# The two layer norms that follow attention take one set of statistics, and the rows of the second are made one tile at a time between the softmax tiles

## The chip, the cores and the metric

The kernel runs on one core of a Trainium2 chip. The metric is the device time of one execution in microseconds (us); less is better. TensorE (PE) does the matrix products and transposes, VectorE (DVE), ScalarE (ACT) and GpSimd (POOL) the elementwise work, and SyncE (SP) issues most of the DMA transfers. Each engine runs its own list of instructions in order; the lists meet only in semaphores.

## The reference, cut to what matters

The input is 4 images of 256 channels and 1024 positions (tokens). Three stages follow each other: a group norm with self-attention, an attention between tokens with residual MLPs, and a mixture of experts (8 experts, 2 for each token).

```python
x = _L0_conv_ref(x, ...)                  # group norm, softmax attention, + xn
t = _to_tokens(x)                         # 4 x 1024 tokens x 256
t = t + _L1_attn_ref(_ln_t(t), ...)       # "t1" below: tokens + second attention
t = t + _L1_ffn_ref(_ln_t(t), ...)        # the experts

def _L1_ffn_ref(x, ...):                  # x = _ln_t(t1), "x2" below
    x_norm = _layernorm(x, ln_g, ln_b)    # "xf" below: norm of a norm, times g, plus b
    ...                                   # gate, top 2 of 8, experts on x_norm
    return x + out
```

Both norms take mean and variance over the 256 channels of a token and add 1e-5 to the variance. The result is t1 + x2 + out, so two things leave this part for every token: the row t1 + x2, to which the experts' outputs are added in memory, and the row xf, from which the gate is computed and which the experts gather.

## The kernel before

All fp32 products are made in three passes of a high and a low part (`three`, L1545), so most of TensorE's time lies in that one helper line. The tile is 128 tokens x 256 channels; an image has 8 tiles (NT).

The function `image(b, first, last)` exists once for each engine. For image b it runs: eight parts of projections (`project`), then softmax 1 over 8 tiles, then a phase R of 24 parts (`R`: kinds "u", "p", "v", the MLPs and projections of the second attention), then softmax 2 over 8 tiles. Image 0 is written out, images 1 and 2 are a hardware loop (`Fori`), image 3 is written out again. In softmax 1 TensorE does in step i: `turn1(i)` (8 transposes of the exponentials), `scores(i + 2)`, `mix1(i - 1)`. VectorE does in step i: `lo1(i)` (low part of the transposed exponentials), `max1(i + 2)`, `out1(i - 1)` (result row, its own norm statistics), `norm1(i - 2)`. ScalarE does `hi1(i)` and `exp1(i + 2)`. GpSimd raises the variance of each tile to the power -0.5 (`first_norm`).

The norms after the second attention of image b - 1, the "tail", have no phase of their own: their pieces are put between the softmax 1 steps of image b, and behind image 3 they stand alone. The pieces before:

- `tail_add` (DVE, L1200): tok = tok + attention, from PSUM.
- `tail_stats(b, which, h)` (DVE, L1211 to L1216) for four tiles (half h) of norm `which`: bn_stats, bn_aggr, then variance + eps.
- `scale` (POOL, L586, L611, L612): power -0.5 of four values, mean times that, times -1.
- `tail_norm` (ACT, L749): four activations that write x2 (norm 0) or xf (norm 1).
- `stream` (POOL, L618): r_out = tok + x2; `affine` (POOL, L623, L625): xf times g_row, plus b_row, four tiles an instruction. For the last image two DVE instructions for each half do the affine part (L1435, L1438).

They are placed by the tables `ACT_TAIL = {1: (0, 1), 3: (1, 0), 4: (1, 1)}` and `DVE_TAIL = {2: (1, 0), 3: (1, 1)}` (step: norm, half), and by `image` for norm 0. In ScalarE's list the first tail piece stands ahead of `hi1(0)` and `exp1(1)`. SP sends r_out and xf to memory (L479, L482), and behind them in its queue loads the next image into xn (L471). In phase R TensorE transposes xf at part 10 (`gate_turn`, L1578) and computes the gate at parts 13 to 16 (`gate`, L1587).

After image 3, DVE, ACT, POOL, SP and PE all wait for each other (`ends`) before the routing begins (L995 on DVE, L666 on POOL). SP joins when both transfers of the last image have landed.

Of the kernel before, what the change touches and what calls it, by code (L numbers as in the profile page):

```python
# [29 lines left out]
P = 128  # L30
# [20 lines left out]
def hybrid_block_kernel(nc, x, q_w, k_w, v_w, oT, q_b, v_b, out_b, gn, W1, W2T, a_qk, a_vT, Wout,  # L51
# [31 lines left out]
    with ctx:  # L83
# [19 lines left out]
        minus_one = sb("minus_one", [P, 8])  # L103
# [43 lines left out]
        tl_bn = bs("tl_bn", [P, 2, NT, 6])  # L147
        tl_mv = bs("tl_mv", [P, 2, NT, 2])
        tl_eps = bs("tl_eps", [P, 2, NT])
        tl_r = bs("tl_r", [P, 2, NT])  # L150
        tl_mr = bs("tl_mr", [P, 2, NT])
        tl_nb = bs("tl_nb", [P, 2, NT])
# [18 lines left out]
        x2 = sb("x2", [P, NT, C], F32, here)  # L171
# [154 lines left out]
        x2_done = signal("x2_done")  # L326
        xf_norm = signal("xf_norm")
# [80 lines left out]
        ACT_TAIL = {1: (0, 1), 3: (1, 0), 4: (1, 1)}  # L408
        DVE_TAIL = {2: (1, 0), 3: (1, 1)}
# [27 lines left out]
        def _(sp):  # L437
# [123 lines left out]
        def _(pool):  # L561
# [11 lines left out]
            make(g.memset(minus_one[:, :], -1.0))  # L573
# [22 lines left out]
            TL_OWN = 8 + 2  # L596

            def last_norms(b, between_norms, affines=True):

                n = [0]  # L600

                def own_step(ins):
                    n[0] += 1
                    ins.then_inc(tl_own, 1)
                    pool.wait_ge(tl_own, at(b, TL_OWN, n[0]))

                def scale(which, h):
                    c = slice(4 * h, 4 * h + 4)
                    pool.wait_ge(tl_in, at(b, 4, 2 * which + h + 1))
                    own_step(rsqrt(tl_r[:, which, c], tl_eps[:, which, c]))  # L610
                    own_step(g.tensor_tensor(tl_mr[:, which, c], tl_mv[:, which, c, 0], tl_r[:, which, c], ALU.mult))  # L611
                    g.tensor_tensor(tl_nb[:, which, c], tl_mr[:, which, c], minus_one[:, 0:4],  # L612
                                    ALU.mult).then_inc(tl_out, 1)

                def stream(h):
                    c = slice(4 * h, 4 * h + 4)
                    pool.wait_ge(x2_done, at(b, 2, h + 1))
                    g.tensor_tensor(r_out[:, c, :], tok[:, c, :], x2[:, c, :], ALU.add).then_inc(r_ready, 1)  # L618

                def affine(h):  # L620
                    c = slice(4 * h, 4 * h + 4)
                    pool.wait_ge(xf_norm, at(b, 2, h + 1))
                    own_step(g.tensor_tensor(xf[:, c, :], xf[:, c, :],  # L623
                                             g_row[:, :].unsqueeze(1).to_broadcast((P, 4, C)), ALU.mult))
                    g.tensor_tensor(xf[:, c, :], xf[:, c, :],  # L625
                                    b_row[:, :].unsqueeze(1).to_broadcast((P, 4, C)), ALU.add).then_inc(xf_ready, 1)

                scale(0, 0)
                scale(0, 1)
                if affines:  # L630
                    stream(0)
                    stream(1)
                between_norms(0)
                between_norms(1)
                scale(1, 0)
                between_norms(2)
                scale(1, 1)
                if not affines:
                    stream(0)
                    stream(1)  # L640
                else:
                    affine(0)
                    between_norms(3)
                    affine(1)
                assert n[0] == TL_OWN or not affines

            def image(b, first, last):
                if not first:
                    last_norms(b - 1, lambda i: first_norm(b, i))
                for i in range(0 if first else 4, NT):  # L650
                    first_norm(b, i)
# [8 lines left out]
            last_norms(B - 1, lambda i: None, affines=False)  # L660
# [64 lines left out]
        def _(act):  # L725
# [18 lines left out]
            def tail_norm(b, which, h):  # L744

                src, dst, ready = ((tok, x2, x2_done), (x2, xf, xf_norm))[which]
                act.wait_ge(tl_out, at(b, 4, 2 * which + h + 1))
                for j in range(4 * h, 4 * h + 4):
                    ins = a.activation(dst[:, j, :], src[:, j, :], ACT.Identity,  # L749
                                       bias=tl_nb[:, which, j:j + 1], scale=tl_r[:, which, j:j + 1])  # L750
                ins.then_inc(ready, 1)
# [6 lines left out]
            def image(b, first, last):  # L758
# [44 lines left out]
                else:  # L803
                    tail_norm(b - 1, 0, 0)
# [67 lines left out]
            for which in range(2):  # L872
                for h in range(2):
                    tail_norm(B - 1, which, h)
            for h in range(2):
                gate_columns(B - 1, h)
            act.wait_ge(xf_col, 2 * B)
# [1028 lines left out]
CONSTANTS = 8  # L1906
# [44 lines left out]
```

## Time and profile before

| | |
|---|---|
| median of 3 runs | 1255.43 us (1252.72 to 1256.72) |
| the profiled execution | 1255.06 us, of which the span of the trace is 1253.2 us |
| PE busy | 1154.5 us (92%) |
| DVE / ACT / POOL busy | 822.1 / 545.5 / 342.7 us |
| images, their softmaxes and phases R | 0 to 693 us |
| tail of image 3 alone, gate, top 2 | 693 to 728 us |
| routing | 728 to 776 us |
| experts and output | 776 to 1253 us |

A row of the timeline gives start, length, engine, line, operation, output and inputs with their shapes, and in brackets how long the engine stood idle before it and what ended that. Instructions of an engine overlap by a little, so the start of the next one can lie before the end of the one before. Matmul ends are modelled.

### The profile page before, as it was taken

Reading aid. Unit: us, or ns where it says so; the run is one execution under the profiler, and the core shown is the slowest. Engines: PE = TensorE matmul, PEld = TensorE weight load, DVE = VectorE, ACT = ScalarE, POOL = GpSimd, SP = SyncE. Lnnn points to the kernel's source line nnn. Section 1 sums busy time; section 2 is a strip of 40 time slices with the busy share of each in tenths; the row PEclk is TensorE's granted clock in tenths of the full one; section 3 lists DMA queues with packets and bytes.
Section 4 is the critical chain, followed back from the end, with each engine's and each line's share of the span. In section 5 each row is a group of like instructions: output and inputs, shape, how many; then the busy total and the mean of one; then the engine's idle time right before and its main releaser. Section 6 shows DMA issues by size and latency. Waiting matters only on the chain.

```text
span 1253.2 us, 25051 instructions
## 1 busy us (share of the span) xinstructions
PE 1154.5 (92%) x8118; PEld 1075.5 (86%) x8119; DVE 822.1 (66%) x1883; ACT 545.5 (44%) x995; POOL 342.7 (27%) x352
## 2 busy tenths in 40 slices
PE   6999999999999999999999335999999999999993
PEld 5897998988988889989888234899999999999992
DVE  4675475954667744768436777796797678856651
ACT  2533445432435334454334313674574556644431
POOL 0010002500004300025000325355455455555440
PEclk9999999999999999999999658899999999999996
DMA  5000000200001100011000133363563547533238
GB/s 164 1 4 31 1 1 1 69 34 1 1 2 35 68 1 1 1 35 35 1 1 1 62 112 106 104 198 53 170 201 52 155 90 216 147 59 54 55 46 273
DMA packets 66207, 82.70 MB, mean 66 GB/s; under 512 B 11105, under 2 KB 56545, under 8 KB 66145
## 3 DMA queue, kind: packets, MB, share of 16 engines
q1 hardware_dynamic: 52128, 63.48, 15.6%
q0 software_dynamic: 14016, 18.37, 8.2%
q8 instruction: 42, 0.69, 0.2%
q14 instruction: 21, 0.16, 0.0%
HBM read 60.85 MB, written 22.02 MB: 66 GB/s over the span
## 4 chain that ended last, share of the span: by engine, by line
PE 81%; DVE 8%; DMA 4%; issue 3%; SPq 1%; ACT 1%; DVEq 1%; POOL 0%; ACTq 0%; POOLq 0%
PE ps L1545 74%; PE ps L1625 2%; DMA w1r<-in_w 2%; PE ps L1587 1%; PE ps L1835 1%; PE ps L1558 1%; DMA rows<-acc_rows 1%; DVE w2s L1466 1%; DVE hs L1512 1%; DVE one_hot L1095 1%; DVE pick_hi L1103 1%; PE ps L1578 1%; PE ps L1634 1%; PE ps L1647 1%; DVE pick_lo L1098 1%
## 5 line engine op out<-in xcount | busy, mean ns | idle before, releaser
L1545 PE MATMUL ps<-xt,w1s 128*128 128x256 f32 x1746 | 257.8, 284 | 1.5 <-DVE xt L1476 1.5
L1545 PE MATMUL ps<-w2s,hs 128*128 128x256 f32 x1728 | 251.1, 280 | 2.8 <-DVE hs L1514 2.7
L1545 PEld LDWEIGHTS ps<-xt,w1s 128*128 128x128 f32 x1746 | 227.7, 190 | 2.1 <-DVE xt L1476 1.9
L1545 PEld LDWEIGHTS ps<-w2s,hs 128*128 128x128 f32 x1728 | 223.6, 188 | 4.2 <-issue 4.1
L944 ACT ACTIVATE h<-ps,b1t 128x256 f32<-128x256 f32 x288 | 137.3, 477 | 114.0 <-PE ps L1545 79.0
L704 POOL DMA_INDIRECT acc_rows<-y_w,now_s x72 | 119.8, 1665 | 166.2 <-issue 155.1
L1512 DVE CAST hs<-h 128x256 fp32r<-128x256 f32 x288 | 91.0, 316 | 71.0 <-ACT h L944 35.9
L1514 DVE TENSOR_TENSOR hs<-h,hs 128x256 fp32r<-128x256 f32 x288 | 123.0, 427 | 9.9
L1545 PE MATMUL ps<-xs,wh 128*128 128x512 f32 x384 | 123.1, 401 | 1.5 <-issue 1.5
L586 POOL TENSOR_TENSOR tl_r<-tl_eps,minus_half 128x4 f32<-128x4 f32 x16 | 16.2, 1014 | 350.8 <-DVE tl_eps L1216 350.8
L691 POOL DMA_INDIRECT xg<-xf_rows,now_g x76 | 93.2, 1226 | 47.3 <-POOL now_g L687 34.7
L1545 PE MATMUL ps<-vs,pr 128*128 128x256 f32 x768 | 98.1, 283 | 0.0
L1545 PEld LDWEIGHTS ps<-vk,pr 128*128 128x128 f32 x768 | 94.0, 188 | 3.2 <-DVE pr L1357 0.8
L1545 PE MATMUL ps<-xs,qs 128*128 128x512 f32 x384 | 95.5, 397 | 0.0
L1545 PE MATMUL ps<-vk,pr 128*128 128x256 f32 x768 | 94.8, 279 | 0.6 <-DVE pr L1357 0.6
L1545 PE MATMUL ps<-qs,ks 128*128 128x512 f32 x384 | 92.3, 391 | 0.0
L1545 PEld LDWEIGHTS ps<-vs,pr 128*128 128x128 f32 x768 | 92.2, 188 | 0.0
L1352 DVE TENSOR_REDUCE neg_max<-ps 128x1 f32<-128x1024 f32 x32 | 39.2, 1225 | 79.7 <-PE ps L1545 79.7
L1545 PEld LDWEIGHTS ps<-xs,wh 128*128 128x128 f32 x384 | 69.7, 189 | 16.0 <-issue 1.7
L1545 PEld LDWEIGHTS ps<-qs,ks 128*128 128x128 f32 x384 | 70.1, 188 | 13.5
L1545 PEld LDWEIGHTS ps<-xs,qs 128*128 128x128 f32 x384 | 69.8, 188 | 13.6
L1545 PE MATMUL ps<-xs,wl 128*128 128x512 f32 x192 | 76.2, 397 | 0.0
(213 smaller groups left out, 1871.5 us busy)
## 6 DMA issues: line engine op xcount, KB each, us to landing
w1r<-in_w SPq DMA_DIRECT2D x16, 1024.0 KB, 5.1
w2r<-in_w SPq DMA_DIRECT2D x16, 1024.0 KB, 8.9
b2t<-in_b SPq DMA_DIRECT2D x36, 128.0 KB, 2.9
xn<-in_x SPq DMA_DIRECT2D x4, 1024.0 KB, 4.9
acc_rows<-r_out SPq DMA_DIRECT2D x4, 1024.0 KB, 4.5
xf_rows<-xf SPq DMA_DIRECT2D x4, 1024.0 KB, 4.9
rows<-acc_rows SPq DMA_DIRECT2D x8, 512.0 KB, 7.4
out_tokens<-cols_out SPq DMA_DIRECT2D x8, 512.0 KB, 9.0
```

The lines of the kernel that those rows point to most:

```text
L586: return g.tensor_tensor(dst, src, minus_half[:, 0:src.shape[1]], ALU.pow)
L691: g.indirect_dma_start(out=xg[:, n, h, :], out_offset=None, in_=xf_d, in_offset=bass.IndirectOffsetOnAxis(ap=now_g[:, n, h:h + 1], axis=0) ...
L704: g.indirect_dma_start(out=acc_d, out_offset=bass.IndirectOffsetOnAxis(ap=now_s[:, n, h:h + 1], axis=0), in_=y_w[:, n, h, :], in_offset=No ...
L944: a.activation(h32[:, gi % 4, :], bank(gi % 4, STEP), ACT.Gelu, bias=b1t[:, n, f:f + 1]).then_inc(h_act, 1)
L1095: v.tensor_tensor(one_hot[:, j, :], iota[:, 0:COLS].unsqueeze(1).to_broadcast((P, PICK, COLS)), hi_f[:, k, t].unsqueeze(2).to_broadcast((P ...
L1098: v.tensor_tensor(pick_lo[:, j, :], iota[:, :].unsqueeze(1).to_broadcast((P, PICK, P)), lo_f[:, k, t].unsqueeze(2).to_broadcast((P, PICK, P)),
L1103: v.tensor_tensor(pick_hi[:, j, 1, :], one_hot[:, j, :], top_w[:, k, t].unsqueeze(2).to_broadcast((P, PICK, COLS)), ALU.mult).then_inc(pic ...
L1352: v.tensor_reduce(neg_max[:, i:i + 1], bank(2 * (i % 2), count=2), AXX, ALU.max, negate=True).then_inc(s2_max, 1)
L1512: v.tensor_copy(hs[0][:, f, :], h32[:, gi % 4, :]).then_inc(h_hi, 1)
L1514: v.tensor_tensor(hs[1][:, f, :], h32[:, gi % 4, :], hs[0][:, f, :].bitcast(F32), ALU.subtract).then_inc(h_lo, 1)
L1545: ins = t.matmul(out, left[l], right[r], start=first and n == 0, stop=last and n == 2, **more)
L1625: ins = t.transpose(bank(4, count=2)[:, j * P:(j + 1) * P], prob[:, i % 2, j * P:(j + 1) * P], ident[:, :])
```

## The change

The statistics of the second norm are worked out from those of the first. With variance v, the norm of the norm scales (t1 - mean) by 1/sqrt(v + eps) and again by 1/sqrt(v/(v + eps) + eps); the product is (v(1 + eps) + eps^2)^-0.5. So both reciprocal roots come from one GpSimd instruction over 8 values (`tail_scales`). `tail_stats` runs for one norm only and has two more small instructions, `tail_xf` makes one tile of xf on DVE in two instructions, and `tail_rows` makes r_out = t1 * (1 + r) - mean * r on ACT in one activation for each tile. `tail_add` writes t1, a tile of its own. x2, `stream`, `affine` and the second round of statistics are gone.

```diff
-        ACT_TAIL = {1: (0, 1), 3: (1, 0), 4: (1, 1)}
-        DVE_TAIL = {2: (1, 0), 3: (1, 1)}
+        DVE_TAIL = {1: (0,), 2: (1,), 3: (2,), 4: (3,), 5: (4,), 6: (5,), 7: (6, 7)}
...
# SP
-                sp.wait_ge(xf_ready, at(b, 2, 2))
+                sp.wait_ge(xf_ready, at(b, NT, NT))
...
# POOL
+            def tail_scales(b, h):
+                c = slice(4 * h, 4 * h + 4)
+                pool.wait_ge(tl_in, at(b, 2, h + 1))
+                g.tensor_tensor(tl_r[:, :, c], tl_eps[:, :, c],
+                                minus_half[:, :].rearrange("p (k t) -> p k t", k=2), ALU.pow).then_inc(tl_own, 1)
+                pool.wait_ge(tl_own, at(b, 2, h + 1))
+                g.tensor_tensor(tl_nb[:, c], tl_nm[:, c], tl_r[:, 0, c], ALU.mult).then_inc(tl_out, 1)
+                g.tensor_tensor(tl_s[:, c], tl_r[:, 0, c], ones[:, 0:4], ALU.add).then_inc(tl_out, 1)
...
# ACT
+            def tail_rows(b, h):
+                act.wait_ge(tl_out, at(b, 4, 2 * h + 2))
+                if not (isinstance(b, int) and b == 0):
+                    act.wait_ge(tok_out, at(b, 16, 0))
                 for j in range(4 * h, 4 * h + 4):
+                    ins = a.activation(r_out[:, j, :], t1[:, j, :], ACT.Identity,
+                                       bias=tl_nb[:, j:j + 1], scale=tl_s[:, j:j + 1])
+                ins.then_inc(r_ready, 1)
...
-                    tail_norm(b - 1, 0, 0)
+                    tail_rows(b - 1, 0)
                     hi1(0)
                 exp1(1)
...
-                    if not first and i in ACT_TAIL:
-                        tail_norm(b - 1, *ACT_TAIL[i])
+                    if not first and i == 1:
+                        tail_rows(b - 1, 1)
...
             act.wait_ge(xf_out, (B - 1) * 16)
-            for which in range(2):
-                for h in range(2):
-                    tail_norm(B - 1, which, h)
             for h in range(2):
                 gate_columns(B - 1, h)
+            for h in range(2):
+                tail_rows(B - 1, h)
...
# DVE
+                v.tensor_scalar(tl_eps[:, 1, cs], tl_mv[:, cs, 1], 1.0 + LN_EPS, LN_EPS * LN_EPS,
+                                ALU.mult, ALU.add)
+                v.tensor_scalar(tl_nm[:, cs], tl_mv[:, cs, 0], -1.0, None, ALU.mult)
+                v.tensor_scalar(tl_eps[:, 0, cs], tl_mv[:, cs, 1], LN_EPS, None, ALU.add).then_inc(tl_in, 1)
+            def tail_xf(b, j):
+                if j % 4 == 0:
+                    dve.wait_ge(tl_own, at(b, 2, j // 4 + 1))
+                if j == 0 and not (isinstance(b, int) and b == 0):
+                    dve.wait_ge(xf_out, at(b, 16, 0))
+                step(v.scalar_tensor_tensor(xf[:, j, :], t1[:, j, :], tl_mv[:, j, 0:1], g_row[:, :],
+                                            ALU.subtract, ALU.mult))
+                settle()
+                v.scalar_tensor_tensor(xf[:, j, :], xf[:, j, :], tl_r[:, 1, j:j + 1], b_row[:, :],
+                                       ALU.mult, ALU.add).then_inc(xf_ready, 1)
...
                 if not first:
                     lo1(0)
-                    tail_stats(b - 1, 0, 1)
...
                     if i + 2 < NT:
                         max1(i + 2)
+                    if not first and i == 0:
+                        tail_stats(b - 1, 1)
                     if i >= 1:
                         out1(i - 1)
                     if i >= 2:
                         norm1(i - 2)
                     if not first and i in DVE_TAIL:
-                        tail_stats(b - 1, *DVE_TAIL[i])
+                        for j in DVE_TAIL[i]:
+                            tail_xf(b - 1, j)
...
                 if not first:
-                    w(xf_ready, 2, 0)
                     w(tok_out, 16, 0)
...
# DVE behind image 3
             tail_add(B - 1, 0)
-            tail_stats(B - 1, 0, 0)
+            tail_stats(B - 1, 0)
             tail_add(B - 1, 1)
-            tail_stats(B - 1, 0, 1)
-            tail_stats(B - 1, 1, 0)
+            tail_stats(B - 1, 1)
+            for j in range(NT):
+                tail_xf(B - 1, j)
             tops(range(0, NT))
-            tail_stats(B - 1, 1, 1)
             tops(range(NT, 2 * NT))
...
```

The wait of `out1(0)` for r_ready is gone too. In TensorE's list only the counts of `xf_ready` differ.

## Rows read from the trace of the kernel before

**Rows 1.** The page, its part 4: chain that ended last, shares by engine.
```profile
PE 81%; DVE 8%; DMA 4%; issue 3%; SPq 1%; ACT 1%; DVEq 1%; POOL 0%; ACTq 0%; POOLq 0%
```

**Rows 2.** Waits of PE over the span: us in total, times, longest.
```profile
PE ps L1578 <- DVE xf L1438: 21.9, 2, 21.5
```

**Rows 3.** Timeline, image 1, the start of softmax 1.
```profile
203.33 1.02 POOL L586 TENSOR_TENSOR tl_r<-tl_eps,minus_half 128x4 f32<-128x4 f32 x1 [70.81 <-DVE tl_eps L1216]
204.95 2.08 ACT L749 ACTIVATE x<-tok,tl_nb,tl_r 128x256 f32<-128x256 f32 x4 [1.39 <-POOL tl_nb L612]
...
207.96 1.23 DVE L1250 TENSOR_TENSOR pr<-ps,pr 128x1024 fp32r<-128x1024 f32 x1 [0.99 <-ACT pr L785]
...
209.33 1.07 PE L1625 MATMUL ps<-ident,prob 128*128 128x128 f32 x8
```

**Rows 4.** The power instruction by tile: ns min/median/max, first and last start.
```profile
L586 POOL TENSOR_TENSOR ln_r<-ln_eps,minus_half x32: 549/646/663, 55.4 to 593.2; 128x1 f32<-128x1 f32 x32
L586 POOL TENSOR_TENSOR tl_r<-tl_eps,minus_half x16: 1007/1017/1020, 203.3 to 706.4; 128x4 f32<-128x4 f32 x16
```

**Rows 5.** DVE's groups by line and shape, 200 to 720 us: busy, mean ns.
```profile
L1369 DVE SCALAR_TENSOR_TENSOR vk<-v,row_inv,vk 128x256 fp32r<-128x256 f32 x24 | 11.6, 484 | 0.9
```

**Rows 6.** Timeline, image 1, the end of softmax 1 and the start of phase R.
```profile
243.01 0.42 DVE L1259 TENSOR_TENSOR tok<-ps,o_row 128x256 f32<-128x256 f32 x1 [0.37 <-PE ps L1545]
...
246.92 0.42 DVE L1259 TENSOR_TENSOR tok<-ps,o_row 128x256 f32<-128x256 f32 x1
...
248.65 0.41 DVE L1273 TENSOR_SCALAR tn<-tok,ln_mv,ln_r 128x256 f32<-128x256 f32 x1
...
248.96 1.22 DVE L1279 TENSOR_TENSOR xs<-ps,xs 128x1024 fp32r<-128x1024 f32 x1
...
250.10 1.22 DVE L1250 TENSOR_TENSOR pr<-ps,pr 128x1024 fp32r<-128x1024 f32 x1
...
254.72 0.42 DVE L1259 TENSOR_TENSOR tok<-ps,o_row 128x256 f32<-128x256 f32 x1
...
259.05 0.69 DVE L1335 TENSOR_TENSOR us<-prob,us 128x512 fp32r<-128x512 f32 x1
...
260.14 0.63 PE L1545 MATMUL ps<-xs,wh 128*128 128x512 f32 x2
```

**Rows 7.** The chain that ended last, in order of time: start, us, what.
```profile
275.19 1.75 PE ps L1578 x16
```

**Rows 8.** A DMA issue of the page (KB, us to landing); one us by windows.
```profile
acc_rows<-r_out SPq DMA_DIRECT2D x4, 1024.0 KB, 4.5
...
221.00:222.00 1.00, 1.00 (x11) 1.00 (x10) 1.00 (x3) 0.00 (x0) 0.39 (x1) 1.00 1.04 346
```

**Rows 9.** Timeline behind image 3 (two rows); then one group by tile.
```profile
707.91 5.63 POOL L618 TENSOR_TENSOR r_out<-tok,x 128x1024 f32<-128x1024 f32 x2
...
708.00 3.34 DVE L1435 TENSOR_TENSOR xf<-xf,g_row 128x1024 f32<-128x1024 f32 x1
...
L687 POOL COPY now_g<-gather_at x38: 184/748/1239, 775.3 to 1203.6; 128x2 int32 x34, 128x2 int32<-128x2 int32 x4
```

**Rows 10.** Timeline, the tail behind image 3, until the routing begins.
```profile
693.39 1.29 DVE L1200 TENSOR_TENSOR tok<-ps,tok 128x512 f32<-128x512 f32 x2 [3.92 <-PE ps L1545]
...
696.65 1.28 DVE L1200 TENSOR_TENSOR tok<-ps,tok 128x512 f32<-128x512 f32 x2
...
699.82 0.17 DVE L1216 TENSOR_SCALAR tl_eps<-tl_mv 128x4 f32<-128x4 f32 x1
...
713.63 0.37 SPq L479 DMA_DIRECT2D acc_rows<-r_out  x1
...
717.07 1.97 PE L1578 MATMUL ps<-ident,xf 128*128 128x128 f32 x8 [0.36 <-DVE xf L1438]
...
719.08 1.01 ACT L755 COPY xfT<-ps 128x1024 f32<-128x1024 f32 x1 [1.32 <-PE ps L1578]
...
728.13 0.24 POOL L666 IOTA iota_i<- 128x128 int32 x1 [14.59 <-DVEq L1445]
```

More of the change, by code:

```diff
@@ L145, in hybrid_block_kernel @@
         ln_r = bs("ln_r", [P, NT])
-        tl_bn = bs("tl_bn", [P, 2, NT, 6])
-        tl_mv = bs("tl_mv", [P, 2, NT, 2])
+        tl_bn = bs("tl_bn", [P, NT, 6])
+        tl_mv = bs("tl_mv", [P, NT, 2])
+        tl_nm = bs("tl_nm", [P, NT])
         tl_eps = bs("tl_eps", [P, 2, NT])
         tl_r = bs("tl_r", [P, 2, NT])
-        tl_mr = bs("tl_mr", [P, 2, NT])
-        tl_nb = bs("tl_nb", [P, 2, NT])
+        tl_nb = bs("tl_nb", [P, NT])
+        tl_s = bs("tl_s", [P, NT])
         xf = bs("xf", [P, NT, C])
@@ L170, in hybrid_block_kernel @@
         here.close()
-        x2 = sb("x2", [P, NT, C], F32, here)
+        t1 = sb("t1", [P, NT, C], F32, here)
         r_out = sb("r_out", [P, NT, C], F32, here)
@@ L572, in _ @@
             make(g.memset(minus_half[:, :], -0.5))
-            make(g.memset(minus_one[:, :], -1.0))
             pool.wait_ge(c_made, made[0])
@@ L594, in first_norm @@
                 rsqrt(ln_r[:, i:i + 1], ln_eps[:, i:i + 1]).then_inc(ln_out, 1)
[L596 to L645, printed above, removed]
@@ L647, in image @@
             def image(b, first, last):
                 if not first:
-                    last_norms(b - 1, lambda i: first_norm(b, i))
-                for i in range(0 if first else 4, NT):
+                    for h in range(2):
+                        tail_scales(b - 1, h)
+                for i in range(NT):
                     first_norm(b, i)
@@ L659, in _ @@
             image(B - 1, False, True)
-            last_norms(B - 1, lambda i: None, affines=False)
+            for h in range(2):
+                tail_scales(B - 1, h)
             pool.wait_ge(tl_out, 4 * B)
@@ L871, in _ @@
             act.wait_ge(xf_out, (B - 1) * 16)
-            for which in range(2):
-                for h in range(2):
-                    tail_norm(B - 1, which, h)
             for h in range(2):
                 gate_columns(B - 1, h)
+            for h in range(2):
+                tail_rows(B - 1, h)
             act.wait_ge(xf_col, 2 * B)
@@ L1198, in tail_add, with tail_stats @@
                 for m in (2 * h, 2 * h + 1):
-                    tile = tok[:, 2 * m:2 * m + 2, :].rearrange("p j c -> p (j c)")
-                    ins = v.tensor_tensor(tile, bank(4 + m), tile, ALU.add)
+                    j = slice(2 * m, 2 * m + 2)
+                    ins = v.tensor_tensor(t1[:, j, :].rearrange("p j c -> p (j c)"), bank(4 + m),
+                                          tok[:, j, :].rearrange("p j c -> p (j c)"), ALU.add)
                 ins.then_inc(added2, 1)
-            def tail_stats(b, which, h):
-                if which:
-                    dve.wait_ge(x2_done, at(b, 2, h + 1))
-                else:
-                    dve.wait_ge(added2, at(b, 2, h + 1))
-                src = (tok, x2)[which]
+            def tail_stats(b, h):
+                dve.wait_ge(added2, at(b, 2, h + 1))
@@ L1209, in tail_stats @@
                 c = range(4 * h, 4 * h + 4)
+                cs = slice(4 * h, 4 * h + 4)
                 for i in c:
-                    step(v.bn_stats(tl_bn[:, which, i, :], src[:, i, :]))
+                    step(v.bn_stats(tl_bn[:, i, :], t1[:, i, :]))
                 settle_aggr()
                 for i in c:
-                    step(v.bn_aggr(tl_mv[:, which, i, :], tl_bn[:, which, i, :]))
+                    step(v.bn_aggr(tl_mv[:, i, :], tl_bn[:, i, :]))
                 settle()
-                v.tensor_scalar(tl_eps[:, which, 4 * h:4 * h + 4], tl_mv[:, which, 4 * h:4 * h + 4, 1], LN_EPS,
-                                None, ALU.add).then_inc(tl_in, 1)
+                v.tensor_scalar(tl_eps[:, 1, cs], tl_mv[:, cs, 1], 1.0 + LN_EPS, LN_EPS * LN_EPS,
+                                ALU.mult, ALU.add)
@@ L1256, in out1 @@
                     w(av_mm, NT, i + 1)
-                    if i == 0 and not first:
-                        w(r_ready, 2, 0)
                     step(v.tensor_tensor(tok[:, i, :], bank(6 + i % 2)[:, C:2 * C], o_row[:, :], ALU.add))
@@ L1292, in image @@
                 if not first:
-                    tail_stats(b - 1, 0, 0)
+                    tail_stats(b - 1, 0)
                 project_lo(6)
@@ L1903, in _ @@
                 ins.then_inc(o_mm, 1)
-CONSTANTS = 8
-OWN_IMAGE = 102
+CONSTANTS = 7
+OWN_IMAGE = 94
 def kernel(**inputs):
```

19 lines of the change are left out of this document (1 added, 18 removed).

## The prediction, made before the changed kernel ran

> **What bounds the kernel now.** I read the chain that ended last first: four fifths of the span are TensorE [rows 1], so within the images another engine counts only where it makes TensorE late. Next I read TensorE's waits: the largest one that this change can touch is the 21.5 us behind image 3, where TensorE has nothing left to do and waits for the last tile rows of xf [rows 2]. That gives two places to work out. First, the tail behind image 3, a serial chain in which each microsecond saved is one saved, until another chain is the longer one. Second, the three images that carry a tail between their softmax steps (1, 2 and 3). There TensorE runs without a gap, so no work taken from the other engines gains anything; work put ahead of something TensorE waits for can only lose. I therefore went through the timeline of image 1 for the points with the least slack: the start of softmax 1 [rows 3] and its end [rows 6]. The same pieces stand in images 2 and 3.
>
> **What is removed within the images, at no gain.** POOL loses six instructions of over 2 us each an image (two beside each other took 5.63 [rows 9]), ACT eight of its 16 activations (about 0.5 us each, by four in 2.08 us [rows 3]), DVE eight statistics, and out1(0) its wait for r_out. None of it stood before TensorE, and what hid it was TensorE's own queue. The constant that is gone from the start is not on the path either.
>
> **The start of softmax 1, +0.70 us an image.** ACT's list is tail piece, hi1(0), exp1(1); TensorE's second turn needs exp1(1) and lo1(0), and starts at 209.33, 0.14 us after lo1(0) has ended [rows 3]: no slack. The tail piece now starts later. The power instruction takes 8 values instead of 4. One value takes 0.55 us alone and four take 1.02, 0.155 a value [rows 4], so 8 values take 1.64 us (+0.62) if that goes on; the bounds are nothing more, if the 8 go together, and twice 1.02. tail_stats has two more tiny instructions ahead of the signal, bounded by 0 (overlapped) and 0.17 each (tl_eps) [rows 10]; I take 0.08 each, +0.16. Behind the power there are two instructions as before, now without a wait between them: -0.08. Sum +0.70. ACT's four activations, hi1(0), exp1(1), lo1(0) and the turn all move by it, and 0.70 is lost, three times. What else waits for the later ACT piece has slack: tail_rows for the second half stands ahead of exp1(3), which TensorE needs two steps later.
>
> **The middle steps, 0.** A tail_xf is two scalar_tensor_tensor instructions, each 0.48 as the one with SBUF inputs [rows 5]; with 0.04 for the wait between them and 0.08 overlap a tile takes 0.92 us. A step of DVE is then lo1 with its reciprocal 1.2, max1 of the same width 1.2, out1 1.73, norm1 0.31, tail_xf 0.92: 5.4 us (lo1 at 250.10, out1 from 246.92 to 248.65, norm1 to 248.96) [rows 6]. TensorE needs more for a step with scores: at its end DVE stood idle for TensorE until out1(4) at 243.01 [rows 6], with a longer statistics piece in some steps. So DVE is in time in steps 1 to 5; the last two have no scores and are the short ones.
>
> **The end of softmax 1, +1.65 us an image.** Here two tiles come at once, and DVE has no idle time. Image 1, in the times of the trace of before: out1(4) 243.01, and with 1.73, norm1 0.32 and tile 4 (0.92), lo1(6) starts at 245.98. With its reciprocal 247.18; out1(5) 248.91; norm1(4) 249.23; tile 5 250.15; lo_tn(0) takes 1.14 (248.96 to 250.10 [rows 6]), so lo1(7) starts at 251.29, where it was 250.10. It ends at 252.51, out1(6) runs to 254.22, norm1(5) to 254.54, tiles 6 and 7 to 256.38, norm1(6) to 256.70. So out1(7) starts at 256.70 instead of 254.72. From there to the end of the second low part of u were 5.02 us (254.72 to 259.05 + 0.69 [rows 6]): 261.72. TensorE's part 4 needs just this and started at 260.14, with 0.4 us to spare. It now starts at 261.8: 1.65 lost. Part of it shows earlier, since mix1(7) needs lo1(7), and DVE's chain sets the sum. What is queued behind: the activations of u and parts 5 to 7, which have slack again. On SP, xf leaves only with its last tile and the load of the next image stands behind it: 256.5, plus 4.5 and 4.5 for two transfers of 1 MB [rows 8], lands at 265.6. The group statistics read it at part 10 of phase R, where TensorE was at 275.19 [rows 7]: hidden by 9 us. Without that cover each microsecond more would stop TensorE in group_average.
>
> **DVE and POOL at the same SBUF tiles, +0.5 us an image.** This is the unknown price. In the tail before, a DVE instruction with two SBUF inputs, as wide as lo1 with its 1.22 [rows 6], took 3.34. It began beside the first of two POOL instructions and ended at 711.34, about when 2.4 for that one and 1.1 for its own work have passed: it stood still while POOL ran [rows 9]. tail_xf has two SBUF inputs and runs right after each out1 has handed its variance to POOL's power instruction. The other way round, a POOL copy of two values, 0.18 at the least, has a median of 0.75 in the expert phase, where DVE is busy, so the small one can also be the one that waits [rows 9]; the power instruction, 0.55 alone, mostly takes 0.65 beside norm1 [rows 4]. Bounds: nothing, or DVE standing still for what is left of the power instruction (0.41) at tiles 4, 5 and 6, 1.2 us an image. I take the small instruction as the one that waits, until tile 7 is done; then norm1(6) needs its result and comes 0.5 late.
>
> The page "SBUF — State Buffer" of the Trainium skill, section "Who interferes with whom", speaks against this change: a DVE instruction with two SBUF inputs and a GpSimd one that reads SBUF exclude each other for their whole length, and the one that came second "fully blocks". By that rule it is the upper bound, 1.2 instead of 0.5, the third rival below; the trace agrees for long instructions (3.34 for 1.22), and for a power instruction no row here shows it.
>
> **The tail behind image 3, -4.75 us.** The first half of add and statistics took 693.39 to 696.65; the second has its tl_eps at 699.82 [rows 10]. With 0.17 more in each half, tl_eps ends at 700.3 and tile 0 starts at 700.25. Eight tiles of 0.92 end at 707.7 (the first four at 704.0, earlier than TensorE wants them). The second four transposes began at 717.07 and so now at 707.75. From there on gate, top 2 and the rest of DVE's list move together by 9.3, and the routing could start at 718.8 instead of 728.13 [rows 10]. It can't, because SP joins there too. ACT makes the copies for the gate first (PE 707.75 + 1.97, copy 1.01, to 710.75 [rows 10]) and only then the eight activations of r_out, 4.1 us, to 714.8. SP issues r_out at 714.9 (before: 713.63), and xf right behind it, while before it left only with the last rows of xf at 717.1. One transfer of 1 MB lands after 4.5 us, of which 3.03 move data at 346 GB/s [rows 8]; two at once need 4.5 + 3.03: 722.4. With 0.25 for the signal the routing starts at 722.65: 5.5 gained of 9.3. The same clash with POOL is larger here, since the power instruction of the second half (1.64) runs beside tile 0: between 0 and 1.5. I take half, 0.75. Leaves 4.75. From the routing on everything only moves.
>
> **Sum.** Images 3 x (0.70 + 1.65 + 0.5) = 8.55; tail -4.75; together +3.8 us. Against the profiled execution's 1255.06 that is 1258.9; that execution lies 0.4 below the median of the three runs, which is nothing beside their spread of 4 us.
>
> **The rivals.**
> 1. *DVE's list at the end of softmax 1 is hidden.* If TensorE doesn't wait at part 4 (because the tiles cost less than 0.92, or its slack is larger than 0.4), the images lose only 2.1 and the tail gains 4.75 to 5.5: 1255.06 - 3.0 = 1252. For it: nothing but that the slack is a difference of two modelled times. Against: two tiles are 1.84 us, and DVE has no gap there to take them up.
> 2. *The transfers don't hold the routing.* If the pair lands by 719, the tail gains 9.3 less 0.75, and the sum is 8.55 - 8.55: 1255. Against: 2 MB at 346 GB/s are 6.1 us.
> 3. *The lock is whole.* Each power instruction holds DVE: 3 x (0.70 + 1.65 + 1.23) = 10.75, and in the tail 1.5 is lost, -4.0: +6.7, 1261.8. It ends clearly slower. It decides where a tail_xf directly follows an out1 whose variance POOL is working on, in tiles 4 to 6, and from 0.2 us a tile on the change is slower than can be put down to chance.
> 4. *The tail doesn't get shorter*, because what is after it (signals, the transfers, POOL's list) is as late as before: 8.55 alone, less than 1 us gained, 1263. The change then doesn't do what it says at the one place where it could. Against: the DVE chain is plainly 9 us shorter.
>
> With no clash at all but the rest as worked out, 3 x 2.35 - 5.5 = +1.55: 1256.6, the low side of my own case.
>
> **How the numbers follow.** My case 0.52, its own range 1256.0 to 1260.5; rival 1 0.13; rival 2 0.07; rival 3 0.22; rival 4 0.06. About 0.3% (3.8 us) is what a measurement of this kernel can tell from no change, and my own sum lies on that edge. Slower by more than it: half of my case 0.25, rivals 3 and 4, together 0.49, rounded down to 0.46 since a term may be double. Faster by more: below 1251.3, a third of rival 1 and some allowance, 0.10. Within: 0.44. The range goes from 1252.0, the middle of rival 1, to 1263.0, past rival 3.
>
> **What would show it.** Step 1: in images 1 to 3 the power instruction takes 1.6, and the turn after it starts 0.7 later after its scores than before. Step 2: TensorE has a wait at L1545 of part 4 or mix1(7) for DVE, 1.6 to 2.9 an image together, nowhere else in the images. Step 3: scalar_tensor_tensor of xf has a mean of 0.48; if it is above 0.55 the lock is at work, and single ones of 0.9 would name tiles 4 to 6. Step 4: behind image 3 the second transposes start near 708 to 709 and POOL's iota is released by SP, not by DVE, near 722.7 less the shift of the images. What would make it wrong: no wait of TensorE at all within the images, or a routing that is released by DVE.

## The result and the profile after

| | before | after |
|---|---|---|
| median, us | 1255.43 (1250.61 to 1258.69, 7 runs) | 1263.15 (1261.14 to 1263.47, 7 runs) |
| ratio after / before | | 1.0063, 95% interval 1.004 to 1.0086 |
| profiled execution, us (span) | 1255.06 (1253.2) | 1263.34 (1261.3) |
| PE / DVE / ACT / POOL busy, us | 1154.5 / 822.1 / 545.5 / 342.7 | 1162.1 / 819.9 / 530.1 / 290.9 |

The change makes the kernel 7.7 us slower. The prediction was 1258.9, with a range up to 1263.0: the sign was right, half the size was missing.

I cut both traces at the same three events: TensorE's first `turn1` of image 0, the first `tail_add` behind image 3, and POOL's iota that opens the routing. Rows of the windows view: stretch, its length, then busy time (and instructions) of PE, PE's weight loads, DVE, ACT and POOL, the granted clock, the DMA share and GB/s. Before:

```profile
42.99:693.39 650.40, 647.80 (x4093) 579.45 (x4091) 402.88 (x833) 262.90 (x385) 81.43 (x89) 1.00 0.05 16
693.39:728.13 34.74, 10.54 (x48) 10.07 (x48) 26.30 (x145) 10.32 (x18) 11.24 (x15) 0.53 0.18 61
728.13:1253.20 525.07, 463.37 (x3818) 457.58 (x3818) 370.24 (x867) 255.38 (x567) 247.45 (x235) 0.94 0.47 124
```

After:

```profile
43.33:705.45 662.12, 654.43 (x4093) 584.21 (x4091) 405.21 (x832) 252.03 (x361) 34.50 (x53) 1.00 0.04 15
705.45:734.44 28.99, 10.53 (x48) 10.07 (x48) 20.94 (x141) 5.96 (x10) 4.27 (x6) 0.57 0.22 73
734.44:1261.30 526.86, 464.41 (x3818) 457.98 (x3818) 371.08 (x867) 255.25 (x567) 249.60 (x235) 0.95 0.48 124
```

The tail gave 5.75 us back, and the images lost 11.72. The first row of each block shows that this loss has two parts. TensorE's idle time in the images grew from 2.60 to 7.69 us (length less busy time): waits. But its busy time grew too, by 6.6 us, for the same 4093 matmuls at the same granted clock of 1.00 (2.4 GHz). About 1.9 us of that lies in the stretches around the waits, which grew by 7.0 us where only 5.1 are idle; the other 4.7 lie elsewhere in the images, and no step of the prediction contained them. The other 2.1 us lie outside: 0.34 ahead of the first cut and 1.79 in the experts.

TensorE's waits after, those that the trace of before does not have (us in total, times, longest):

```profile
PE ps L1586 <- DVE pr L1220: 2.1, 3, 0.7
PE ps L1506 <- DVE pr L1220: 1.6, 3, 0.5
PE ps L1506 <- DVE us L1304: 1.4, 3, 0.5
```

Each comes three times, once for each image that carries a tail, and together they are the 5.1 us of new idle time. The first is `turn1(1)`, the second `mix1(7)`, the third part 4 of phase R. Here is the first in image 1, timeline (start, us, engine, line, operation, idle before); the rows of before are [rows 3], with one more here, TensorE's first turn. Before, then after:

```profile
205.54 1.03 PE L1625 MATMUL ps<-ident,prob 128*128 128x128 f32 x8
```

```profile
205.03 1.65 POOL L596 TENSOR_TENSOR tl_r<-tl_eps,minus_half 128x8 f32<-128x8 f32 x1 [71.74 <-DVE tl_eps L1175]
...
207.10 1.03 PE L1586 MATMUL ps<-ident,prob 128*128 128x128 f32 x8
207.23 2.08 ACT L707 ACTIVATE r_out<-t,tl_nb,tl_s 128x256 f32<-128x256 f32 x4 [2.12 <-POOL tl_s L600]
...
210.24 1.23 DVE L1220 TENSOR_TENSOR pr<-ps,pr 128x1024 fp32r<-128x1024 f32 x1 [1.72 <-ACT pr L743]
...
211.61 1.06 PE L1586 MATMUL ps<-ident,prob 128*128 128x128 f32 x8 [0.74 <-DVE pr L1220]
```

From the power instruction to ACT's first activation it is 2.20 us, where [rows 3] have 1.62; TensorE's second turn starts 4.51 us after its first (207.10), where before it was 3.79. The other two images show 0.72 and 0.63 more.

The end of softmax 1 in the same image, to be held against [rows 6]. Two more rows of before (turn 7 and the transposes of part `turn_tn(1)`, the next ones that TensorE makes in phase R), then after:

```profile
247.59 1.04 PE L1625 MATMUL ps<-ident,prob 128*128 128x128 f32 x8
...
262.94 1.03 PE L1647 MATMUL ps<-ident,tn 128*128 128x128 f32 x8
```

```profile
250.10 1.04 PE L1586 MATMUL ps<-ident,prob 128*128 128x128 f32 x8
...
254.98 3.14 PE L1506 MATMUL ps<-vs,pr 128*128 128x256 f32 x24 [0.53 <-DVE pr L1220]
...
259.10 0.41 DVE L1227 TENSOR_TENSOR tok<-ps,o_row 128x256 f32<-128x256 f32 x1
...
263.41 0.69 DVE L1304 TENSOR_TENSOR us<-prob,us 128x512 fp32r<-128x512 f32 x1
...
264.16 0.73 PE L1506 MATMUL ps<-xs,wh 128*128 128x512 f32 x2 [0.43 <-DVE us L1304]
...
267.07 1.04 PE L1608 MATMUL ps<-ident,tn 128*128 128x128 f32 x8
```

From turn 7 to the first transposes of part `turn_tn(1)` TensorE took 16.97 us (250.10 to 267.07) where it took 15.35 (247.59 to 262.94): 1.62 more. The other two images lost 1.61 and 1.68. Only 1.0 us of it is idle time (0.53 at `mix1(7)`, 0.43 at part 4). DVE's `out1(7)` comes at 259.10, and from there to the end of the second low part of u (264.10) it is 5.00, where it was 5.02.

The tail behind image 3, to be held against [rows 10]:

```profile
705.45 1.29 DVE L1157 TENSOR_TENSOR t<-ps,tok 128x512 f32<-128x512 f32 x2 [4.06 <-PE ps L1506]
...
712.24 0.48 DVE L1183 SCALAR_TENSOR_TENSOR xf<-t,tl_mv,g_row 128x256 f32<-128x256 f32 x1
...
719.17 0.48 DVE L1186 SCALAR_TENSOR_TENSOR xf<-xf,tl_r,b_row 128x256 f32<-128x256 f32 x1
...
722.62 4.04 ACT L707 ACTIVATE r_out<-t,tl_nb,tl_s 128x256 f32<-128x256 f32 x8
...
734.44 0.23 POOL L623 IOTA iota_i<- 128x128 int32 x1 [19.68 <-SPq L489]
```

and the same stretch in the chain that ended last (start, us, what):

```profile
726.75 0.37 SPq L476
727.23 7.03 DMA xf_rows<-xf
734.44 0.23 POOL iota_i L623
```

DVE has the last top 2 at 730.5, but the routing waits until 734.44 for SP, whose two transfers follow each other from 726.75 on.

### The profile page after: what moved, and what is told of

It reads as the page before. It is cut to its first block, busy times and chain, and to the rows that moved or that the text cites. A ratio compares the mean times of both kernels' runs of the same rounds, so it can differ in the third digit from the quotient of the medians.

```text
span 1261.3 us, 24959 instructions
## 1 busy us (share of the span) xinstructions
PE 1162.1 (92%) x8118; PEld 1080.7 (86%) x8119; DVE 819.9 (65%) x1879; ACT 530.1 (42%) x963; POOL 290.9 (23%) x307
## 4 chain that ended last, share of the span: by engine, by line
PE 72%; DVE 10%; issue 9%; DMA 3%; POOL 2%; ACT 2%; SPq 1%; DVEq 0%; POOLq 0%; ACTq 0%
PE ps L1506 67%; PE ps L1796 1%; PE ps L1519 1%; PE ps L1586 1%; POOL ln_r L582 1%; DMA w1r<-in_w 1%; ACT r_out L707 1%; DVE tl_bn L1167 1%; PE ps L1548 1%; DMA rows<-acc_rows 1%; POOL tl_r L596 1%; DVE w2s L1427 1%; DVE one_hot L1052 1%; DVE pick_hi L1060 1%; PE ps L1539 1%
## 5 line engine op out<-in xcount | busy, mean ns | idle before, releaser
L596 POOL TENSOR_TENSOR tl_r<-tl_eps,minus_half 128x8 f32<-128x8 f32 x8 | 13.3, 1664 | 345.4 <-DVE tl_eps L1175 345.4
```

Of the source, the lines that this page charges most:

```text
L596: g.tensor_tensor(tl_r[:, :, c], tl_eps[:, :, c], minus_half[:, :].rearrange("p (k t) -> p k t", k=2), ALU.pow).then_inc(tl_own, 1)
```

## The experiments

Spans of one part of the kernel come from the profile of each: "images" is the first cut to the second, "tail" the second to the third. The changed kernel and two experiments with the same addresses and the same image code (`e7_clash`, `e5_rows_first`) gave 662.12, 662.40 and 662.45 us for the images, so half a microsecond there can be told apart. Each kernel computes all outputs.

### The addresses of the tiles

Nothing in the diff touches the products of the softmaxes, yet their weight loads are slower. One tile, durations in ns min/median/max. Before, then after:

```profile
L1545 PEld LDWEIGHTS ps<-vk,pr x768: 186/188/193, 152.3 to 692.9; 128*128 128x128 f32 x192
L1545 PE MATMUL ps<-vk,pr x768: 274/280/390, 152.5 to 693.0; 128*128 128x256 f32 x192
```

```profile
L1506 PEld LDWEIGHTS ps<-vk,pr x768: 186/192/193, 153.3 to 705.0; 128*128 128x128 f32 x192
L1506 PE MATMUL ps<-vk,pr x768: 277/283/386, 153.5 to 705.1; 128*128 128x256 f32 x192
```

The products of vs with pr moved alike, 280 to 283 and 188 to 192. 3 ns for each of these 1536 products are 4.6 us, and that is what is left of the images' loss once the waits' places are taken off: 11.72 - 3 x (0.72 + 1.62) = 4.7. What the change does to these tiles is move them. It drops `minus_one` (32 bytes a partition) and makes the tail's small tiles 288 bytes smaller, so `pr` lies 32 bytes lower and `vs` and `vk` 320 bytes lower. Two experiments turn only this.

`e1_layout`, the changed kernel with two unused tiles, so that every large tile lies where it was before:

```
         minus_half = sb("minus_half", [P, 8])
+        sb("pad_a", [P, 8])
...
         tl_s = bs("tl_s", [P, NT])
+        bs("pad_b", [P, 72])
```

> The changed kernel, with two unused tiles (32 bytes and 288 bytes a partition) that put every later SBUF tile back to its address of before. Nothing else differs, and everything is computed. Theory A (addresses): the products of pr with vs and vk go back from a mean weight load of 191 and 192 ns to 188, the 0.8 us that each of the four softmax 2 phases lost and the 0.2 of each softmax 1 come back, about 4 us in all: 1259. Rival B (the code itself, or the chip that day): the loads stay at 191 to 192 and the time at 1263.

`e2_shift`, the kernel before with five small tiles allocated last, so that the large ones lie where the changed kernel has them:

```
-        minus_one = sb("minus_one", [P, 8])
...
-        ln_r = bs("ln_r", [P, NT])
...
-        tl_mv = bs("tl_mv", [P, 2, NT, 2])
...
-        tl_r = bs("tl_r", [P, 2, NT])
-        tl_mr = bs("tl_mr", [P, 2, NT])
...
         hold_r2 = sb("hold_r2", [P, 4096], F32, batch_scope)
+        minus_one = bs("minus_one", [P, 8])
+        ln_r = bs("ln_r", [P, NT])
+        tl_mv = bs("tl_mv", [P, 2, NT, 2])
+        tl_r = bs("tl_r", [P, 2, NT])
+        tl_mr = bs("tl_mr", [P, 2, NT])
```

> The kernel before, instruction for instruction, but with small tiles allocated elsewhere, so that every large SBUF tile has the address it has in the changed kernel. Everything is computed. Theory A (addresses): weight loads of pr go from 188 to 191 and 192 ns, the kernel gets slower by about 4 us: 1259.5. Rival B (the changed code): no difference from the kernel before, 1255.4.

Measured: `e1_layout` 1259.1 us (1257.3 to 1260.41), ratio to before 1.0033 (1.0018 to 1.0047); images 658.05. `e2_shift` 1260.5 us (1256.95 to 1262.94), ratio 1.0038 (1.0019 to 1.0056); images 655.33, tail 34.74 as before. The loads and products, first of `e1_layout`, then of `e2_shift`:

```profile
L1508 PEld LDWEIGHTS ps<-vk,pr x768: 186/188/193, 151.8 to 700.1; 128*128 128x128 f32 x192
L1508 PE MATMUL ps<-vk,pr x768: 274/280/390, 152.0 to 700.2; 128*128 128x256 f32 x192
```

```profile
L1545 PEld LDWEIGHTS ps<-vk,pr x768: 186/192/192, 151.9 to 696.8; 128*128 128x128 f32 x192
L1545 PE MATMUL ps<-vk,pr x768: 277/283/386, 152.2 to 696.9; 128*128 128x256 f32 x192
```

So the addresses alone cost the kernel before 4.9 us in the images (655.33 - 650.40), and giving them back is worth 4.1 to the changed kernel (662.12 - 658.05). TensorE's busy time in the images says the same: 652.87 us in `e2_shift` against 647.80, and 649.66 in `e1_layout` against 654.43, so 5.1 and 4.8 us. The two agree as far as they should: in `e1_layout` TensorE is faster up to `mix1(7)` and part 4 and waits longer there for DVE, 3.6 us over the three images instead of 3.0.

Which address matters? Four more layouts, each timed in one execution only, with unused tiles of other sizes (in `e8_pr_before` also with `ln_r` allocated last):

> The changed kernel with pr at its address of before (143200 bytes) and xf, t1, us, vs, vk at those of the changed kernel (vs at 209984). Everything is computed. If the address of pr decides how long its weight loads take, they are back at 188 ns in the mean. If the address of vs and vk decides (or their distance from pr, which is 66784 here, 67104 before, 66816 in the changed kernel), they stay at 191 to 192.

> The reverse: pr at its address of the changed kernel (143168 bytes), and xf, t1, us, vs, vk at those of before (vs at 210304). Everything is computed. If pr's address decides, its loads stay at 191 to 192 ns; if that of vs and vk decides, they are at 188.

> The changed kernel with pr at its address of before (143200 bytes) and vs at 210400, vk at 218592: no address as in any kernel so far but pr's, and distances of 67200 and 75392 bytes, both multiples of 128, as in the changed kernel (66816, 75008) and in no other. Everything is computed. If the distance modulo 128 decides, weight loads of pr take 191 to 192 ns in the mean; if it is the addresses of the changed kernel themselves, 188.

> The changed kernel with pr at its own address (143168 bytes) and vs at 210272, vk at 218464: distances that leave 32 modulo 128, as in the kernel before (67104). Everything is computed. If the distance modulo 128 decides, weight loads of pr take 188 ns and the 24 products of a softmax 1 step 2.81 to 2.84 us as before; if pr's address has a part of its own, 189 or more.

| kernel | pr at | vs at (vk 8192 on) | distance pr to vs, modulo 128 | images, us |
|---|---|---|---|---|
| after | 143168 | 209984 | 0 | 662.12 |
| `e10_pair128` | 143200 | 210400 | 0 | 661.72 |
| `e8_pr_before` | 143200 | 209984 | 96 | 659.84 |
| `e9_vs_before` | 143168 | 210304 | 64 | 658.73 |
| `e1_layout` | 143200 | 210304 | 32 | 658.05 |
| `e11_pr_after32` | 143168 | 210272 | 32 | 657.74 |

(Addresses in bytes within a partition. Whole times: 1259.71, 1258.16, 1262.27 and 1258.72 us for e8, e9, e10 and e11.) Neither pr's own address nor that of vs orders this table: with pr at 143168 the images take 662.12, 658.73 and 657.74, with vs at 209984 662.12 and 659.84. What does order these six is the distance between the stationary and the moving tile of the product, modulo 128 bytes: 0 is the worst and 32 the best, each in two layouts. The loads of vk,pr have a median of 188 ns in `e8_pr_before`, `e9_vs_before` and `e11_pr_after32`. They have it in `e10_pair128` too, where 191 to 192 were expected if the distance decides. By the mark set for it that experiment missed; what speaks for the distance there is its products, and the time of the images:

```profile
L1508 PEld LDWEIGHTS ps<-vk,pr x768: 186/188/190, 152.3 to 703.8; 128*128 128x128 f32 x192
L1508 PE MATMUL ps<-vk,pr x768: 274/283/387, 152.5 to 704.0; 128*128 128x256 f32 x192
```

(Its products of vs with pr have a median of 281.) In the traces the weight loads run beside the products (in the changed kernel 24 loads from 251.09 to 254.03 and their 24 products from 251.11 to 254.23). That the two reads get in each other's way is only a guess: the runs show that addresses decide, and an order by distance in six layouts, but not the mechanism. The tiles between (us, xf) moved along with vs, and why `e10_pair128` has fast loads with slow products is open. The Trainium skill, page "TensorE: Matmul & The Clock Gate", section "Step-by-step: what each phase is for", says that TensorE has two independent read ports into SBUF, so that loading the next weights takes nothing from the running matmul. The trace agrees as far as the two run side by side; that they both get 3 or 4 ns longer when only their tiles are moved isn't in that sentence, and whether the ports have a part in it no run here shows.

### The end of softmax 1

`e3_spread`: the same eight tiles of xf, placed where DVE has room.

```
-DVE_TAIL = {1: (0,), 2: (1,), 3: (2,), 4: (3,), 5: (4,), 6: (5,), 7: (6, 7)}
+DVE_TAIL = {1: (0,), 2: (1, 2), 3: (3, 4), 4: (5, 6), 5: (7,)}
```

> The changed kernel with the tiles of xf made two at a time in steps 2 to 4 and the last one in step 5, so that none stands in steps 6 and 7 of softmax 1. Everything is computed. Theory A (DVE's list at the end of softmax 1 is what TensorE waits for): the 1.6 us that TensorE loses there in each of images 1 to 3 are gone, 3 x 1.6 = 4.9 us less than the changed kernel, about 1258. Rival B (the loss is somewhere else in the piece, or DVE is too full in steps 2 to 4 with 6.3 of 6.7 us): the loss moves to the middle steps and the time stays within 1 us of 1263.

Measured: 1257.28 us (1256.27 to 1260.28), ratio 1.0018 (1.0002 to 1.0034). The timeline of image 1, TensorE's turn 7 and the transposes of part `turn_tn(1)`:

```profile
248.74 1.04 PE L1586 MATMUL ps<-ident,prob 128*128 128x128 f32 x8
...
264.23 1.03 PE L1608 MATMUL ps<-ident,tn 128*128 128x128 f32 x8
```

This is 15.49 us, against 16.97 in the changed kernel and 15.35 before. The waits for `pr` at `mix1(7)` and for `us` at part 4 are gone, and the images shrank to 657.84, by 4.3. Of the 1.62 us an image 1.48 were thus the place of the xf tiles in DVE's list, not their work (with the old addresses as well, in `e6_all` below, the stretch is 15.37): two of them in one step cost TensorE nothing in the steps 2 to 4, where it also has scores to compute.

### The start of softmax 1

`e4_order`: ACT's tail piece behind `hi1(0)` and `exp1(1)` instead of ahead of them.

```
-                    tail_rows(b - 1, 0)
                     hi1(0)
                 exp1(1)
+                if not first:
+                    tail_rows(b - 1, 0)
```

> The changed kernel with ScalarE's first piece of the tail (four rows of r_out) behind hi1(0) and exp1(1) instead of ahead of them. Everything is computed. Theory A (this piece and the longer power instruction before it delay the second turn): the 0.72 us in each of images 1 to 3 is gone, and the 0.2 that were already there before, 2.1 to 2.7 us less: about 1261. Rival B (the turn waits for something else, such as DVE's two more small instructions): less than 0.5 us changes.

Measured: 1259.87 us (1258.3 to 1262.93), ratio 1.0044 (1.0027 to 1.006). ACT and TensorE in image 1:

```profile
206.24 1.03 PE L1587 MATMUL ps<-ident,prob 128*128 128x128 f32 x8
...
207.31 1.02 ACT L743 CAST pr<-ps 128x1024 fp32r<-128x1024 f32 x1 [3.06 <-PE ps L1587]
...
209.32 2.08 ACT L707 ACTIVATE r_out<-t,tl_nb,tl_s 128x256 f32<-128x256 f32 x4
...
209.85 1.04 PE L1587 MATMUL ps<-ident,prob 128*128 128x128 f32 x8
```

The second turn now starts 3.61 us after the first (206.24), less than the 3.79 of before, and 3.62 in the other two images. The power instruction still takes 1.65 us, but nobody that TensorE needs waits for it. Images 658.97, 3.15 less than in the changed kernel; from the turns alone 2.6 were due (0.90, 0.88 and 0.80), and the other half microsecond was not traced.

### The lock between DVE and POOL

In the changed kernel the power instructions and DVE's two-input instructions do run beside each other, and DVE's don't stand still:

```profile
L596 POOL TENSOR_TENSOR tl_r<-tl_eps,minus_half x8: 1637/1646/1809, 205.0 to 712.4; 128x8 f32<-128x8 f32 x8
L1183 DVE SCALAR_TENSOR_TENSOR xf<-t,tl_mv,g_row x32: 476/479/486, 220.3 to 718.7; 128x256 f32<-128x256 f32 x32
L1186 DVE SCALAR_TENSOR_TENSOR xf<-xf,tl_r,b_row x32: 484/485/487, 220.9 to 719.2; 128x256 f32<-128x256 f32 x32
```

(By tile: ns min/median/max.) All 64 of DVE's instructions take 0.48 us, those in the tail beside the power instruction of 712.41 too; that one takes 1.81 instead of 1.65. To see whether the long wait of [rows 9] was such a clash at all, `e7_clash` puts one long POOL instruction with SBUF inputs beside the same DVE list, behind image 3. What it writes is used by nothing.

```
             for h in range(2):
                 tail_scales(B - 1, h)
+            g.tensor_tensor(prob[:, 0, :].rearrange("p (j c) -> p j c", c=C), tok[:, 0:4, :], tok[:, 4:8, :],
+                            ALU.mult).then_inc(tl_own, 1)
+            pool.wait_ge(tl_own, 2 * B + 1)
```

> The changed kernel with one GpSimd product more (two SBUF inputs of 128 x 1024, result not used) behind its last power instruction, so that it runs beside tiles 2 to 7 of xf behind image 3. All outputs are computed as before. Theory A (a long GpSimd instruction shuts out a DVE one with two SBUF inputs, a power instruction of few values doesn't): one scalar_tensor_tensor of xf takes 2.4 to 2.9 us instead of 0.48, xf is done 2.4 later and so is the routing (31.4 instead of 29.0 us after the first tail_add). Rival B (this DVE instruction is never shut out): all stay at 0.48 and the GpSimd one takes longer itself, routing at 29.0.

Measured, timeline behind image 3:

```profile
711.49 1.81 POOL L596 TENSOR_TENSOR tl_r<-tl_eps,minus_half 128x8 f32<-128x8 f32 x1 [1.32 <-DVE tl_eps L1178]
711.83 0.48 DVE L1189 SCALAR_TENSOR_TENSOR xf<-xf,tl_r,b_row 128x256 f32<-128x256 f32 x1
...
713.79 2.55 POOL L618 TENSOR_TENSOR prob<-tok 128x1024 f32<-128x1024 f32 x1
714.06 2.56 DVE L1186 SCALAR_TENSOR_TENSOR xf<-t,tl_mv,g_row 128x256 f32<-128x256 f32 x1
716.66 0.48 DVE L1189 SCALAR_TENSOR_TENSOR xf<-xf,tl_r,b_row 128x256 f32<-128x256 f32 x1
```

The DVE instruction that starts 0.27 us behind the long one takes 2.56 us and ends 0.28 after it: it stood still for 2.08 us, and the tail is longer by just that (31.09 instead of 28.99; the whole 1264.04 us, in one execution). In the same execution the power instruction, 1.8 us long, held nobody. So both readings of [rows 9] have their place: a long POOL instruction over many values shuts DVE out, one over eight values a partition doesn't. The rule of the Trainium skill that the prediction weighed (page "SBUF — State Buffer", section "Who interferes with whom") fits the first to 0.2 us (DVE ended 0.28 us behind POOL, with 0.48 of its own work) and not the second: the length of the POOL instruction is not what DVE loses.

### The order behind image 3

`e5_rows_first`: ACT makes r_out ahead of the gate's copies.

```
+            for h in range(2):
+                tail_rows(B - 1, h)
             for h in range(2):
                 gate_columns(B - 1, h)
-            for h in range(2):
-                tail_rows(B - 1, h)
```

> The changed kernel with one edit behind image 3: ScalarE makes the eight rows of r_out ahead of its two copies for the gate, in time in which it stood idle. Everything is computed. Theory A (the two transfers of the last image hold the routing): r_out leaves some 10 us earlier and lands before xf, xf leaves with its last tile, and the routing is released by DVE instead of SP, 3.7 us earlier (30.8 instead of 34.4 us after the point where TensorE goes idle is the wrong count; in terms of the tail: 29.0 becomes 25.3 us): about 1259.5. Rival B (another engine is as late as SP, or the copies for the gate come late behind the rows): 29.0 stays.

Measured: 1259.03 us (1257.57 to 1261.05), ratio 1.0029 (1.0013 to 1.0045). Timeline:

```profile
717.23 0.37 SPq L476 DMA_DIRECT2D acc_rows<-r_out  x1
...
720.02 0.37 SPq L479 DMA_DIRECT2D xf_rows<-xf  x1
...
731.04 0.23 POOL L623 IOTA iota_i<- 128x128 int32 x1 [16.01 <-DVEq L1406]
```

The first transfer goes out before DVE's tiles are finished, and the routing waits for DVE and no longer for SP. The tail is 25.32 us, 3.67 less than in the changed kernel and 9.42 less than before. The prediction had 9.3 for DVE's chain alone.

### All of it together

`e6_all` has the pads, the spread tiles, ACT's order in softmax 1 and the order behind image 3.

> All four together on the changed kernel: addresses of before, xf tiles two at a time in steps 2 to 4, ScalarE's first piece behind exp1(1), rows of r_out first behind image 3. Everything is computed. If the four causes add (4 to 5 us, 4.3 to 4.9, 2.1 to 2.7, 3.7) the images take no longer than before or 0.6 us less, and the tail 25.3 instead of 34.7 us: 9 to 10 us less than the kernel before, ratio 0.992 to 0.993. If two of them are the same cause, or a new wait takes their place, less than 6 us.

Measured: 1249.43 us (1246.08 to 1251.76, 9 runs), ratio 0.9952 (0.993 to 0.9974). It is faster than the kernel before (median 1254.40 us, measured beside it), and 13.7 us below the changed one. But 9 to 10 us, a ratio of 0.992 to 0.993, had been expected, and by the medians it is 5.0: the images and the tail came out as expected, the whole did not. The windows with the same cuts:

```profile
43.84:694.32 650.48, 647.66 (x4093) 579.74 (x4091) 407.05 (x832) 251.94 (x361) 34.51 (x53) 1.00 0.05 16
694.32:719.64 25.32, 10.53 (x48) 10.07 (x48) 20.96 (x141) 6.18 (x10) 4.27 (x6) 0.55 0.25 84
```

The images take what they took before, 650.48 against 650.40, and the waits for `pr` and `us` in softmax 1 and at part 4 are gone. The three edits alone were worth 4.1, 4.3 and 3.15 us there, 11.5 together, and all three 11.6: all that the change lost in the images is accounted for. The gain is the tail's 9.4 us, of which 7.4 reach the span of the profiled execution (1245.8 against 1253.2): the first cut lies 0.85 later here and the experts took 1.1 more. The first cut lay between 41.90 and 43.84 us over all these kernels, with no edit ahead of it but addresses and one constant. Why the medians show only 5.0 is open; the kernel before has executions from 1250.93 to 1259.18 beside it.

## Why the prediction was right or wrong

The sum of the spans, as measured: +0.34 (start) +2.07 (`turn1(1)`, three images) +4.91 (end of softmax 1, three images) +4.74 (the rest of the images: addresses) -5.75 (tail) +1.79 (experts) = +8.1. The prediction had +3.8.

- **Removed work, no gain: right.** POOL lost 52 us of busy time and ACT 15; neither is seen in a gain of the images.
- **Start of softmax 1, +0.70: right**, 0.72, 0.72 and 0.63. The power instruction took 1.65 (predicted 1.64), and `e4_order` shows that the order in ACT's list is what makes it cost anything.
- **Middle steps, 0: right.** No wait of TensorE lies there. `e3_spread` shows even two tiles a step hidden in the steps 2 to 4.
- **End of softmax 1, +1.65: right**, 1.62, 1.61 and 1.68, with the waits where they were predicted. Their idle time is 1.0 an image and not the 1.6 named as the sign; the rest of the stretch's growth stands as busy time. Rival 1 falls.
- **The clash, +0.5 an image and 0.75 in the tail: wrong, it is 0.** This term came from [rows 9], where the POOL instruction was over 2 us long with 1024 values a partition; I carried it over to one of eight values, with half the bound as price. `e7_clash` shows the lock for the one and none for the other. Rival 3 (the whole lock) falls with it: its 1261.8 lay near the result for a reason that isn't there.
- **Tail, -5.5 ahead of the clash: right**, -5.75. The two transfers landed 7.5 us after the first issue, as worked out (4.5 + 3.03), and the routing was released by SP. `e5_rows_first` shows the 9.3 behind it. Rivals 2 and 4 fall.
- **The step that failed is one that wasn't there.** With the clash at 0 my own sum is the +1.55 that the prediction gave as its low side, and the parts that it covers measured +1.2. What was missing is 4.7 us in the images, more than all its error by the spans (+8.1 against +3.8). The prediction treated the removal of `minus_one` as free ("not on the path either") and the new tile sizes not at all. It looked at each instruction that is added or removed, and at none that is only moved in memory. `e1_layout` and `e2_shift` show this cost from both sides.
- **The experts' +1.8 stay open.** The eleven experiments gave 525.4 to 527.0 us for that stretch, and before had 525.07. They lean with the addresses and with the changed code: the changed code took 526.2 to 527.0 at distance 0 (six kernels) and 525.6 to 526.2 in the other layouts (five), the old code in `e2_shift` 525.4. Each is one execution, whole executions of the kernel before differ by 8 us, and no run was made for it.
- **The range** left out addresses altogether, and its upper end was set by a rival that turned out empty. It missed by 0.15 us.
- **The chances** were added up wrongly: half of my case and rivals 3 and 4 are 0.25 + 0.22 + 0.06 = 0.53 for clearly slower, where the prediction has 0.49.

## What to carry to other kernels

Taking away or shrinking a small tile moves every tile allocated behind it: compare the medians of the weight loads and products that the diff doesn't touch, and hold the addresses with a pad before judging the edit. Put new pieces of work not at equal distances but where the engine that is waited for has room, and never ahead of the instruction that the bounding engine needs next. In a serial tail, look who joins last: here the gain of DVE's list was cut by two transfers that an idle ACT let go 10 and 7.5 us later than it could (in `e5_rows_first` they are issued 11.5 and 14.3 us into the tail, in the changed kernel 21.3 and 21.8).

## What was not expected of the hardware

- The duration of an fp32 product of 256 columns went from 280 to 283 ns and that of its weight load from 188 to 192 (medians of 768) when its two tiles moved from a distance of 32 to one of 0 modulo 128 bytes (`e2_shift`; in another layout with distance 0, `e10_pair128`, the load stayed at 188). Over 1536 such products that was 4 to 5 us of 650.
- A power instruction on POOL takes 0.55 us for one value a partition, 1.02 for four [rows 4] and 1.65 for eight, and no DVE instruction with two SBUF inputs was longer beside it; POOL's own was, by 0.16. A POOL product of 1024 values a partition held such a DVE instruction for 2.08 us.
- Two transfers of 1 MB, the second issued 0.48 us behind the first, landed 7.03 us after the issue of the second, where one alone takes 4.5 [rows 8].
